# First layer's attention: head mask as TensorE weights, scores in 32-partition groups, all products on VectorE

## The reference, cut to what matters

```python
    T, B, C = x.shape                      # 8, 256, 128
    qkv = x @ in_proj_w.T + in_proj_b
    q, k, v = jnp.split(qkv, 3, axis=-1)   # each reshaped to (T, B, 16, 8)
    scores = jnp.einsum('tbhd,sbhd->bhts', q, k) * scale
    attn = jax.nn.softmax(scores, axis=-1)
    ctx = jnp.einsum('bhts,sbhd->tbhd', attn, v).reshape(T, B, C)
    attn_out = ctx @ out_w.T + out_b
    h = _layernorm(x + attn_out, ln1_g, ln1_b)
```

## Time and profile before

| | |
|---|---|
| three executions | 878.33, 878.42, 881.91 us; median 878.42 |
| profiled execution, span from first to last instruction | 921.0 us; its only time shown |
| busy in it: TensorE, VectorE, ScalarE, GpSimd | 692.4 (75%), 595.3 (65%), 399.3 (43%), 292.5 us (32%) |
| mean granted TensorE clock | 0.87 of 2.4 GHz |

### The profile page before, as it was taken

The page is one execution under the profiler, slowest core; times in us unless marked ns, Lnnn a source line. Parts: engine busy times, 40 slices in busy tenths (PEclk is TensorE's granted clock), DMA queues, the critical chain, the costliest instruction groups (busy, mean ns, idle before and its releaser), DMA issues. The chain is left out here.

```text
span 921.0 us, 14463 instructions
## 1 busy us (share of the span) xinstructions
PE 692.4 (75%) x4255; PEld 516.3 (56%) x4255; DVE 595.3 (65%) x1590; ACT 399.3 (43%) x990; POOL 292.5 (32%) x303
## 2 busy tenths in 40 slices
PE   4999866743979379328986988999976677749991
PEld 2999834632767248327875674656544444426560
DVE  4797487538688611286667567889947665636685
ACT  3201334534735123164444446767756333326660
POOL 1373143540000265300100002445410555665552
PEclk9999878865799779768997899999997699969996
DMA  9991001220100140319008431222100122112515
GB/s 286 244 281 77 1 27 44 68 69 0 47 0 1 11 47 9 93 51 391 1 1 156 124 86 34 75 78 73 53 25 17 48 61 60 57 54 57 163 58 141
DMA packets 79564, 72.97 MB, mean 79 GB/s; under 512 B 9618, under 2 KB 73885, under 8 KB 78977
## 3 DMA queue, kind: packets, MB, share of 16 engines
q1 hardware_dynamic: 68000, 57.56, 23.3%
q0 software_dynamic: 7072, 12.40, 5.2%
q10 hardware_dynamic: 4416, 2.10, 0.9%
HBM read 42.85 MB, written 27.46 MB: 76 GB/s over the span
## 5 line engine op out<-in xcount | busy, mean ns | idle before, releaser
L3493 POOL DMA_INDIRECT ys<-work,back_to x78 | 78.9, 1011 | 83.7 <-DVE work L3452 38.0
L3336 PE MATMUL banks<-weights,work 128*128 x156 | 91.6, 673 | 7.8 <-issue 6.2
L2535 DVE TENSOR_REDUCE work<-banks 128x2 f32<-128x512 f32 x128 | 83.5, 683 | 14.4 <-PE banks L2526 13.1
L3349 PEld LDWEIGHTS banks<-consts,work 128*128 128x128 f32 x156 | 21.8, 155 | 79.4 <-issue 52.5
L3359 PE MATMUL banks<-weights,work 128*128 x312 | 54.8, 303 | 5.4 <-DVE work L3452 3.2
L3349 PE MATMUL banks<-consts,work 128*128 128x128 f32 x156 | 34.3, 305 | 32.1 <-DVE work L3441 15.5
L816 POOL DMA_INDIRECT xs<-t,idx x48 | 49.1, 1023 | 28.7 <-DMA ys<-work,back_to 15.4
L2526 PE MATMUL banks<-work 96*128 96x256 bf16 x256 | 49.3, 277 | 9.1 <-DVE work L2535 6.0
L1196 POOL DMA_INDIRECT g<-rows,back_to x16 | 15.3, 958 | 120.4 <-DVE back_to L1922 115.8
L3359 PEld LDWEIGHTS banks<-weights,work 128*128 128x128 f32 x312 | 46.2, 213 | 8.1 <-issue 7.7
L2939 PE MATMUL banks<-work 99*128 99x256 bf16 x256 | 48.7, 275 | 1.7 <-issue 1.6
(11 more groups left out here) (508 smaller groups left out, 1946.1 us busy)
## 6 DMA issues: line engine op xcount, KB each, us to landing
weights<-in_w SPq DMA_DIRECT2D x1, 6668.0 KB, 19.6
weights<-in_w SPq DMA_DIRECT2D x1, 4569.5 KB, 33.8
work<-xs SPq DMA_DIRECT2D x62, 64.5 KB
weights<-in_r SPq DMA_DIRECT2D x1, 2950.5 KB, 26.5
xs<-zero SPq DMA_DIRECT2D x1, 2600.0 KB, 26.1
xs<-zero SPq DMA_DIRECT2D x1, 2580.0 KB, 33.5
work<-xs SPq DMA_DIRECT2D x39, 65.0 KB
weights<-in_w SPq DMA_DIRECT2D x1, 2124.5 KB, 12.1
```

Source lines behind the costliest of these rows:

```text
L2535: v.tensor_reduce(self.mxb[:, 2 * h:2 * h + 2], self.n.bank(bank).rearrange("p (r n) -> p r n", r=2), AX, ALU.max, negate=True).then_inc(* ...
L3336: pe.matmul(self.mid(t), self.hT[t % 4], w1[:, bass.ds(off * 4, 512)], start=True, stop=True).then_inc(*self.prod1.up())
L3349: ins = pe.transpose(self.mid(m)[:, 128 * f:128 * f + 128], self.ha[m % 4][:, 128 * f:128 * f + 128], self.c["ident"])
L3493: g.indirect_dma_start(ys[:, :], bass.IndirectOffsetOnAxis(ap=n.back_to[:, t:t + 1], axis=0), self.yb[t % self.RETURNS], None, bounds_chec ...
```

## The change

- The mask `head_at` shrinks from 1,024 columns to 64: two blocks of 32 columns that send channel p to row p // 8, or to row 16 + p // 8. It becomes the stationary operand and the product moves through. Each score product takes four matmuls of 256 columns, one for each key in it, and the four write to four groups of 32 partitions of one bank. Even and odd products (`sg`) share the 32 rows.
- Scores now lie with keys and heads on partitions and the batch along the columns, two positions to a bank. So for each of four groups g ScalarE copies the bank (`act_raw`), TensorE turns it back with four transposes (`pe_turned`), and the softmax runs over 512 columns, one round for two positions. The eight scores of a softmax then lie 16 elements apart.
- VectorE makes all products, in an order written out in `BEFORE_MAX`, `BEFORE_SUM` and `LAST`; GpSimd keeps its four base-row additions. Two bias additions of VectorE move behind its first two products, and the values' matmuls between the products (`VALUES_AFTER`).
- In products 29 and 31 (`HALVED`) VectorE adds the two halves, and TensorE sums four pieces in place of eight.

```diff
+    BEFORE_MAX = ((0, 1, 2, 3, 4, 5, 6), (16, 8, 17), (20, 9, 10, 21, 11, 22, 12, 13, 14), (24, 15, 25, 26))
+    BEFORE_SUM = ((7,), (18, 19), (23,), (27,))
+    LAST = (28, 29, 30, 31)
+    HALVED = (29, 31)
+    VALUES_AFTER = (0, 1, 2, 5)
+    TURNED_AFTER = (4, 7, 22, 25)
...
-    @staticmethod
-    def pooled(k):
-        return k % 16 in (2, 5, 9, 12, 15)
-
...
+    def scores(self, g):
...
+        return self.n.bank(g % 2).rearrange("p (x s h) -> p x s h", x=4, s=8)
+
...
-        buf = self.prods[k % 6]
+        buf = self.buffer(k)
         if k < 16:
             t, sg = k // 2, k % 2
             return buf.rearrange("p (s n) -> p s n", n=NS), self.kT[:, 4 * sg:4 * sg + 4, :], grow(self.qT[:, t, :], 4), ALU.mult
         t, half = (k - 16) // 2, k % 2
-        p = self.sc[t // 4].rearrange("p (a t h s) -> p a t s h", a=2, t=4, s=8)[:, half, t % 4].unsqueeze(3)
+        p = self.sc[t // 2].rearrange("p (x s h) -> p x s h", x=4, s=8)[:, 2 * half + t % 2].unsqueeze(3)
         v = self.v.rearrange("p (s a) c -> p a s c", a=2)[:, half].rearrange("p s (h x) -> p s h x", x=8)
         return buf.rearrange("p (s h x) -> p s h x", s=8, x=8), p.broadcast_to((P, 8, 16, 8)), v, ALU.mult
...
+    def pe_turned(self, g):
+        n, pe = self.n, self.tensor
+        pe.wait_ge(*self.raw.at(g))
+        pe.wait_ge(*(self.shifted.at(g - 2) if g >= 2 else self.vals.at(g + 2)))
+        for half in range(2):
+            for t in range(2):
+                at = NS * t + 128 * half
+                ins = pe.transpose(n.bank(g % 2)[:, 128 * (2 * half + t):128 * (2 * half + t) + 128], self.sc[g][:, at:at + 128], self.c["ident"])
+        ins.then_inc(*self.turned.up())
...
-        for q in range(4):
-            pe.wait_ge(*(self.out(4 + q) if q < 2 else self.vals.at(q - 2)))
...
-        for k in range(32):
-            prod = self.prods[k % 6]
-            pe.wait_ge(*self.made(k))
+        for i, k in enumerate(self.order):
+            prod = self.buffer(k)
...
             if k < 16:
                 t, sg = k // 2, k % 2
-                for half in range(2):
-                    ps = bank(2 + 2 * (t // 4) + half)[:, t % 4 * 128:t % 4 * 128 + 128]
-                    for s in range(4):
-                        at = 128 * (4 * sg + s)
-                        ins = pe.matmul(ps, prod[:, s * NS + half * 128:s * NS + half * 128 + 128], n.w0["head_at"][:, at:at + 128],
-                                        start=(sg + s == 0), stop=(sg == 1 and s == 3))
+                for s in range(4):
+                    ins = pe.matmul(bank(2 + t // 2)[32 * s:32 * s + 32, t % 2 * NS:t % 2 * NS + NS],
+                                    n.w0["head_at"][:, 32 * sg:32 * sg + 32], prod[:, s * NS:(s + 1) * NS], start=(sg == 0), stop=(sg == 1))
             else:
                 tile = k - 16
...
+                terms = 4 if k in self.HALVED else 8
...
             ins.then_inc(*self.used.up())
...
+            if k in self.TURNED_AFTER:
+                self.pe_turned(self.TURNED_AFTER.index(k))
+            if k in self.VALUES_AFTER:
+                self.pe_values(self.VALUES_AFTER.index(k))
...
+    def make(self, k):
+        v, i, ring = self.vector, self.place[k], len(self.prods)
+        if i >= ring:
+            v.wait_ge(*self.used.at(i - ring))
...
+            v.wait_ge(*self.vals.at(3))
+            v.wait_ge(*self.soft.at((k - 16) // 4))
+        if k not in self.HALVED:
+            v.tensor_tensor(*self.product(k)).then_inc(*self.made.up())
+            return
+        v.tensor_tensor(*self.product(k)).then_inc(*self.D.up())
+        v.wait_ge(*self.D.now())
+        prod = self.buffer(k)
+        v.tensor_tensor(prod[:, 0:512], prod[:, 0:512], prod[:, 512:1024], ALU.add).then_inc(*self.made.up())
...
-        make(0, 13)
-        for g in range(2):
...
+        self.biased(1)
+        self.biased(3)
+        for g in range(4):
+            for k in self.BEFORE_MAX[g]:
+                self.make(k)
+                if k < 2:
+                    self.biased(5 + 2 * k)
+            scores = self.scores(g)
+            w = self.sc[g].rearrange("p (x s h) -> p x s h", x=4, s=8)
+            mx, sm = (a.rearrange("p (x h) -> p x h", h=16) for a in (self.mx, self.sm))
+            v.wait_ge(*self.turned.at(g))
+            v.tensor_reduce(mx, scores.rearrange("p x s h -> p x h s"), AX, ALU.max).then_inc(*D.up())
...
-            v.tensor_tensor(w, scores, grow_in(self.mx, 8), ALU.subtract).then_inc(*self.shifted.up())
-            make(*((13, 16), (21, 24))[g])
+            v.tensor_tensor(w, scores, mx.unsqueeze(2).broadcast_to((P, 4, 8, 16)), ALU.subtract).then_inc(*self.shifted.up())
+            for k in self.BEFORE_SUM[g]:
+                self.make(k)
             v.wait_ge(*self.exped.at(g))
-            v.tensor_reduce(self.sm, w, AX, ALU.add).then_inc(*D.up())
+            v.tensor_reduce(sm, w.rearrange("p x s h -> p x h s"), AX, ALU.add).then_inc(*D.up())
             v.wait_ge(*D.now())
...
-            v.tensor_tensor(w, w, grow_in(self.sm, 8), ALU.mult).then_inc(*self.soft.up())
-            if g == 0:
-                make(16, 21)
-        make(24, 32)
-        yield
+            v.tensor_tensor(w, w, sm.unsqueeze(2).broadcast_to((P, 4, 8, 16)), ALU.mult).then_inc(*self.soft.up())
+        for k in self.LAST:
+            self.make(k)
...
+    def act_raw(self, g):
+        a = self.scalar
+        a.wait_ge(*self.used.at(self.place[4 * g + 3]))
+        a.activation(self.sc[g], self.n.bank(2 + g), ACT.Copy).then_inc(*self.raw.up())
...
+    def act_values(self, q):
+        a, n = self.scalar, self.n
+        a.wait_ge(*self.v_mm.at(q))
+        dst = self.v.rearrange("p (g a r) c -> p a g r c", a=2, r=2)[:, q // 2, 2 * (q % 2):2 * (q % 2) + 2]
+        a.activation(dst, n.bank(q % 2).rearrange("p (g r c) -> p g r c", g=2, r=2), ACT.Copy).then_inc(*self.vals.up())
...
+        self.act_values(0)
+        self.act_values(1)
+        self.act_values(2)
+        self.act_raw(0)
+        self.act_values(3)
+        self.act_exp(0)
+        self.act_raw(1)
+        self.act_exp(1)
+        self.act_context(0)
+        self.act_raw(2)
+        self.act_exp(2)
+        self.act_context(1)
+        self.act_raw(3)
+        self.act_exp(3)
+        self.act_context(2)
+        self.act_context(3)
...
     def pool(self):
         n, g = self.n, self.gpsimd
-        for k in range(16):
-            if self.pooled(k):
-                self.make(g, k, self.made_p)
...
-        for k in range(16, 32):
-            if self.pooled(k):
-                self.make(g, k, self.made_p)
...
-        "head_at": np.arange(P)[:, None, None] // 8 * 8 + np.arange(8)[None, :, None] == np.arange(P)[None, None, :],
+        "head_at": np.arange(P)[:, None, None] // 8 + 16 * np.arange(2)[None, :, None] == np.arange(32)[None, None, :],
```

87 lines of the change are left out of this document (40 added, 47 removed).

## The result

The median of 20 runs of the changed kernel is 880.0 us (869.86 to 889.42), that of 20 runs of the kernel before, in the same session, 881.97 us. The ratio is 0.9944, with a 95% interval of 0.9919 to 0.9968: 4.9 us faster, 2.8 to 7.1. The means are then 876.1 and 881.6 us, 5.5 apart (4.4 to 6.6); over all runs they are 878.4 and 881.9, 3.5 apart. The three runs shown ahead of the prediction (median 878.42) were on the low side: the 183 have a median of 881.6 us.

The account below looks back on a forecast made before the run. TensorE was taken to bound the attention stage, with VectorE next: 22.1 + 36.5 + 1.4 + 14.7 + 1.5 + 2.5 + 1.4 = 80.1 against 86.64, so 878.4 - 6.5 = 871.9 us; range 868.0 to 878.0.

Parts of the forecast that it names:

- one to one: From the first output addition to the kernel's end: whatever moves that moment moves the rest, so 6.5 us carries over.
- The forecast of 80.1 for the first output addition: End of the attention stage: VectorE's summed terms put its first output addition at 80.1 us, against 86.64.
- Softmax rounds: VectorE in attention: four rounds over 512 columns at 3.7 us each with gaps, together 14.7 us.
- Waits: VectorE in attention: 1.5 us at the last maximum and 1.0 at the first sum; the end 1.4.
- GpSimd's additions, put at nothing: Four base-row additions on GpSimd: done near 22 us, ahead of VectorE's first product, so costing nothing; otherwise 3.6 us.
- Start: VectorE's first product in attention: follows the second bias addition, starting at 22.1 us.
- Both things that the prediction left out: Before attention: shorter first weight load, worth 0.3 us, and TensorE's earlier clock rise, worth 0 to 1.6 us.
- Groups in a row: Score matmuls on TensorE: the four column groups run serially, 1.79 us per product, giving 882.3 us; chance 0.05.
- The clock falls: TensorE idle near 31 to 38 us loses clock; low stretches cost 2 to 3.5 us, about 874.7; chance 0.10.
- Additions collide: GpSimd's additions meet VectorE's products because row weights land after 22 us: 3.6 us lost, 875.5; chance 0.14.
- Strided maxima: Softmax maxima on VectorE also pay for strided PSUM reads: 1.4 us more, 873.3 us; chance 0.13.
- The warning that the stretch behind the stage might grow: Behind attention: forecast wrong if the first output addition comes near 80 us and the stretch behind it grows; no size.

Follow-up runs that it names:

- the two delays: Changed kernel with its first bias addition on VectorE made three or ten times more: ratios 0.9954 and 1.0034 to the kernel before, means 877.0 and 884.4 us.
- The run with one column group: Changed kernel with all four score matmuls of every odd product sent to partitions 0 to 31: first output addition at 86.17 us, no whole time given.
- the padded runs: Changed kernel with 960 unused zero columns behind the mask, restoring the first weight load's size: ratios 0.9928 and 0.9935 to the kernel before, medians 874.7 and 878.7 us.
- the filler: Changed kernel with thirteen extra 128-column matmuls in TensorE's waits, written to a bank nobody reads yet: ratio 0.9952 to the kernel before.

## Why the prediction was right or wrong

**The number was wrong, 880.0 against 871.9, the range too; the direction was right.** The step that failed is the base in "878.4 - 6.5 = 871.9", and that no room was left for the scatter of a median. The miss of 8.1 us, in parts:

- *The base.* 878.42 was the median of three runs. In the session of the result the kernel before had 881.97, over the study 881.6. This is 3.5 us of the miss, and the prediction kept no allowance for it in the range. The measured ratio on 878.42 gives 873.5, inside the range.
- *The median.* By the ratio the changed kernel is 4.9 us faster, the two medians of 20 differ by 2.0 only. The four groups of the changed kernel have medians of 880.0, 876.0, 877.7 and 876.6 us, so this first one was the highest. That is another 3.0 us, and chance.
- *The gain.* 6.5 forecast, 4.9 by this ratio, 5.2 (3.8 to 6.5) by the four ratios, 5.5 (4.4 to 6.6) by the means. This is the remaining 1.6 us. The step "one to one" from the stage to the end was not refuted: the two delays passed on in full.

**The forecast of 80.1 for the first output addition came near the measured 78.7 to 80.0 by luck.** It is 22.1 for the start and 58.0 for the rest of the stage. The start came at 18.8 to 20.2, about 2.7 us earlier, and the rest took 59.8 to 60.0, 1.9 more. The stage proper gained 4.6 us where the prediction had 6.5. The bound did move from TensorE to VectorE, as forecast, and most terms held:

- Score product: 0.58 taken, 0.57 measured. The run with one column group shows why.
- Products: pace 1.14, as taken. The strided sum 1.03, measured 1.02 (the 0.6 ns per element of its working give 0.31 us for 512 elements, not the 0.35 that it added; the measured addition is 0.34); maxima 0.68, as taken; subtraction and scaling 0.69, reciprocal 0.55, as taken. The Trainium skill's rule on cache lines (Advanced Engine Details and Errata, Memory Cachelines) holds for VectorE's reads of SBUF here, 1.02 us against 0.69. Carried over to its reads of PSUM it did not come true.
- Softmax rounds: 3.7 taken, 3.8 measured (29.27 to 30.59 and 32.97 to 35.43), 0.5 us more over four.
- Waits: 1.5 taken and 1.73 measured at the last maximum, 1.0 and 1.16 at the first sum; the end 1.4 and 1.54. Together 0.5 us more.
- GpSimd's additions, put at nothing: they ran from 16.71 to 21.93 and met the first two products, at 1.92 and 1.45 us, 0.95 us in all. This is the term of the stage that was wrong by most.
- Start: 22.1 taken, 19.14 measured for the end of the second bias addition. Both things that the prediction left out came. The load is shorter, 1.2 us by the padded runs. And TensorE's weight loads last 0.19 us from 15.19 on, which in the earlier trace rows comes between 19.09 and 20.31: the clock rose earlier. That moment scatters in both kernels (16.5, 18.4 and 19.9 us in three profiles before, 14.9 to 17.1 in four after), so how much of the start is the change and how much chance is known only to about 1 us.

**The rivals.** *Groups in a row* did not happen; with half of the products so, the stage took 6.7 us more. *The clock falls* was right in that it fell, near 36 us, and wrong on the price: the buffers hid it, and the filler shows that taking it away gains nothing. *Additions collide* happened in part at the start; their full collision costs 4.3 us more than their early place, where the prediction had 3.6. *Strided maxima* did not happen. The warning that the stretch behind the stage might grow did not come true by more than the scatter: 796.8 us against 795.6.

**What stays open.** The first output addition comes 6.7 us earlier (give or take about 1.2, for the start scatters) and the time falls by 5.2 to 5.5; the intervals overlap, and whether something is lost behind the stage is not shown. The low stretch within the stage is no such loss, since the filler, which has none, is not faster. The mean granted clock of the runs is 0.875 for the changed kernel and 0.882 before, a difference larger than the 0.004 that the one stretch in the stage makes, and the time of a run goes with its clock in both kernels: 869.86 us at 0.887, 889.42 at 0.865. All 56 runs of the changed kernel also scatter more widely than the 183 of the kernel before (standard deviation 5.1 against 3.5 us). Whether the changed stage makes low stretches behind it more frequent, or chance did, these runs do not settle.

## What to carry to other kernels

Count the work that an engine frees and then ask which engine is next: here TensorE gave up some 19 us of score work (16 x 1.22) and the stage proper gained 4.6, because VectorE, alone and with few collisions, needs 60. Where GpSimd and VectorE made such products at the same time, the pair took 3.3 us and VectorE alone would have taken 2.3; measure the pair, not the one. When a forecast moment comes true, check its parts too: here an early start hid a stage that was 1.9 us too long. And before a number is forecast to half a per cent, look at how far medians of a few runs of the same kernel lie apart.

## What the runs showed of the hardware

- Four fp32 matmuls of 32 stationary columns and 256 moving ones take 0.57 us on four groups of output partitions and 1.85 us on one.
- VectorE sums 512 elements from SBUF in 0.69 us when neighbours are summed and in 1.02 when they lie 64 bytes apart; the maximum out of PSUM takes 0.68 at the same distance, and a subtraction that reads PSUM strided 0.69, as before.
- Beside GpSimd's fp32 product of 1,024 elements VectorE's takes 2.7 to 3.4 us instead of 1.22, beside its addition of 512 elements 2.11; a sum over 1,024 elements of one operand was not slowed (1.21 us at 47.18 in the second profile of the kernel before, beside a product of GpSimd from 46.13 to 49.48).
- A stretch of 6.8 us at a mean granted clock of 0.52 cost nothing while VectorE was the bound and six buffers lay between (79.4 us without the stretch, 78.7 to 80.0 with it).
- Nearly the same code, in one kernel, was granted a mean clock of 0.80 or 0.50 over 10 us in two executions.
